# Two causal convolutions as matrix products: narrower loads for the second, split loads for the first, and kernel copies made group by group

## The chip, the cores and the metric

The kernel runs on one core of one Trainium2 chip. The metric is the device time of one execution in microseconds (us). The core has TensorE (PE: matrix products; PEld: its weight loads), VectorE (DVE), ScalarE (ACT), GpSimd (POOL) and SyncE (SP, which here issues transfers), and 16 DMA engines that move data.

## The reference, cut to what matters

```python
q, k, v = (einsum('blh,dh->bdl', u, W) + b for (W, b) in ((Wq, bq), (Wk, bk), (Wv, bv)))
k  = causal_conv(k, k_kernel)  + k_D * k          # first convolution, per channel, 512 taps
kv = k * v
y  = causal_conv(kv, ssm_kernel) + D * kv         # second convolution
x  = layernorm(u + (y * q) @ Wo.T + bo)
h  = square(relu(x @ W_fc.T)); y2 = h @ W_proj.T
x  = layernorm(x + spikes(y2) / 5)                # five threshold steps on y2
```

There are 16 sequences of 512 tokens and 256 channels; the hidden layer has 1024 units. The reference does the convolutions by FFT; only the result is wanted.

## The kernel before, in words

**Convolution as matrix product.** For each channel a causal convolution with 512 taps is a triangular Toeplitz matrix (each row is the row above, moved by one tap). It is never stored whole. A "window" tile of a channel has 128 partitions and 512 columns, and its partition p holds the taps moved right by p; TensorE uses 128 columns of it at a time as weights. Each number is kept as two float16 parts, so a channel has two windows.

**Groups, halves, steps.** The 256 channels are cut into 32 groups of 8 (`NG`, `G`), each in two halves of four channels. Step s of the first stage computes: a quarter (four of the 16 sequences) of the projection of q, k, v for the next 32 channels (line 666, 96 matmuls; not in the last four steps), the first convolution of group s (line 688, 96 matmuls) and the second convolution of group s-1 (line 688, 96 more). TensorE does them in this order.

**Where windows come from.** A prepared row of taps lies in `kpad_dram`, in 16 copies (`NCOPY`) so that 16 partitions can be read at once from different places. `spread(piece)` (line 293) makes the 16 copies from `ksplit_dram` for 32 channels (four groups) at a time: two transfers of 1024 KB, one for each convolution. `load_windows(conv, half, g)` (line 305) reads 64 partitions of one half, each partition from an address one element before its neighbour's: one transfer of 512 KB. VectorE then sets the part above the diagonal to zero (`mask`, line 975), and the other 64 partitions are a copy of the first 64, moved 64 columns to the right. For the first convolution ScalarE makes this copy (line 442; in the last four groups VectorE makes one half, line 983), for the second VectorE does (line 992).

**Buffers.** The first convolution's windows have two places (even and odd groups), the second's one place, and two in the last four groups. So a load for the second convolution waits until the same half of the group before has been used by TensorE (`c2_half`).

**What sets the order.** Each engine has one program, written out in order, and semaphores join them. SP issues all window loads and spreads on one queue. In step s it issues the load of weights and one `spread` (each fourth step, if pieces are left), then, each after its wait, the two first convolution loads of group s+2 (waiting for `c1_half` of group s) and the two second convolution loads of group s (waiting for `c2_half` of group s-1). VectorE's order in step s is: product with q of group s-2 (line 1018), both masks of the first convolution's group s+1, both masks and both copies of the second convolution's group s-1, three reads of the projection (lines 951 and 954), product with v (line 1012). At the start VectorE also splits u into two parts (line 937), between other work, and GpSimd splits two of the eight pieces (line 584).

**The second stage** (output projection, norms, the hidden layer, the spikes) comes after the last step and touches none of the changed lines.

Of the kernel before, what the change touches and what calls it, by code (L numbers as in the profile page):

```python
# [13 lines left out]
P = 128  # L14
B, L, D, F = 16, 512, 256, 1024
# [5 lines left out]
CH = 32  # L21
NC = D // CH
G = 8
GPC = CH // G
NG = D // G
HG = G // 2
HP = P // 2
ROWS = P + D * 2 * L
NCOPY = 16
SLICE = CH * 2 * L  # L30
EARLY = 4
NU = 8
UP = TOK // NU
BOTH = 4
EPS = 1e-5
X1S = 2.0 ** 10
# [35 lines left out]
def build(nc, uT, u, wcat, wk_n, wv_n, bias, bo, k1, k2, kd1, kd2, woT, wfT, wpT, out):  # L72
# [11 lines left out]
    with ExitStack() as ctx:  # L84
# [32 lines left out]
        def part(kb, dt, pattern=None, **dims):  # L117
# [83 lines left out]
            sem(n) for n in ("kpad_zero", "kpad_hi", "kpad_lo", "kpad_head", "ksplit_out", "w16_out"))  # L201
        kpad_out = [sem(f"kpad_out{n}") for n in range(NC)]

# [3 lines left out]
            sem(n) for n in ("t_zero", "c1_masked", "c2_masked", "c1_copied", "c2_copied"))  # L207
        c1_copied_dve, c1_half, c2_half = (sem(n) for n in ("c1_copied_dve", "c1_half", "c2_half"))

# [46 lines left out]
        def shifted(windows):  # L256
# [3 lines left out]
            return t[HP:P, :, HP:L], t[0:HP, :, 0:L - HP]  # L260

# [16 lines left out]
        def _(sp):  # L278
# [5 lines left out]
            for n in range(NU):  # L284
                sp.dma_start(u_st[:, :, n * UP:(n + 1) * UP],
                             uT.rearrange("(t p) n -> p t n", p=P)[:, :, n * UP:(n + 1) * UP]).then_inc(ld_u[n], 16)
            def spread(piece):

                at, n = piece * SLICE, SLICE // NCOPY
                for conv in range(2):  # L290
                    src = ksplit_dram[conv, at:at + SLICE].rearrange("(r n) -> r n", n=n)
                    dst = kpad_dram[conv, :, P + at:P + at + SLICE].rearrange("k (r n) -> r k n", n=n)
                    sp.dma_start(dst, src.unsqueeze(1).to_broadcast([NCOPY, NCOPY, n])).then_inc(kpad_out[piece], 16)

            def load_windows(conv, half, g):


                row = HG * 2 * L
                first = kpad_dram[conv, 0, P + (2 * g + half) * row:]
                if g % GPC == 0 and conv == 0 and half == 0:  # L300
                    sp.wait_ge(kpad_out[g // GPC], 32)
                second_place = conv == 1 and g >= NG - GPC and g % 2 == 0
                slot = 6 + half if second_place else 4 + half if conv else g % 2 * 2 + half
                windows = windows_of(conv, g % PAIR, half, g >= NG - PAIR)
                sp.dma_start(windows[0:HP].rearrange("p c a n -> p (c a n)"),
                             bass.AP(first.tensor, first.offset, [[ROWS - HP // NCOPY, NCOPY], [-1, HP // NCOPY], [1, row]])
                             ).then_inc(t_in[slot], 16)

# [11 lines left out]
            sp.wait_ge(ksplit_out, 32)  # L320
            spread(0)
            sp.wait_ge(kpad_head, 16)
            sp.wait_ge(kpad_out[0], 32)
            for conv, g in ((0, 0), (0, 1), (1, 0)):
                for half in range(2):
                    load_windows(conv, half, g)
            for piece in range(1, EARLY):
                spread(piece)

# [10 lines left out]
            for s in range(NG):  # L340
                chunk = s // GPC + 2
                if s % GPC == 0 and chunk < NC:
                    sp.wait_ge(proj, GPC * (chunk - 1))
                    load_w(chunk, chunk % 2)
                if s % GPC == 0 and s // GPC + EARLY < NC:
                    spread(s // GPC + EARLY)
                if s == NG - GPC:
# [509 lines left out]
        def _(dve):  # L857
# [16 lines left out]

            nc.vector.memset(T[HP:P].rearrange("p k c a n -> p (k c a) n")[:, :, 0:HP], 0.0).then_inc(t_zero, 1)
            link(nc.vector.memset(part_max[:, :], 0.0))

# [85 lines left out]
            def mask(conv, s, g, half):  # L963

                if conv == 0:
                    dve.wait_ge(t_in[s % 2 * 2 + half], 8 * (g - s % 2) + 16)
                elif isinstance(g, int) and g >= NG - GPC:

                    nth = (g - (NG - GPC)) // 2 + 1
                    dve.wait_ge(t_in[4 + half] if g % 2 else t_in[6 + half],  # L970
                                16 * (NG - GPC + nth if g % 2 else nth))
                else:
                    dve.wait_ge(t_in[4 + half], 16 * (g + 1))
                tri = windows_of(conv, s, half, final(g))[0:HP].rearrange("p c a n -> p (c a) n")[:, :, 0:HP]
                nc.vector.tensor_tensor(tri, tri, causal[0:HP, 0:HP].unsqueeze(1).to_broadcast([HP, 2 * HG, HP]),  # L975
                                        ALU.mult).then_inc((c1_masked, c2_masked)[conv], 1)
# [18 lines left out]
            dve.wait_ge(t_zero, 1)  # L995
            for quarter in range(GPC):
# [44 lines left out]
            for s in range(PAIR):  # L1041
                step(s, NG - PAIR, s < GPC, NC - 2)
                if s == GPC - 1:
                    nc.vector.memset(T2[HP:P].rearrange("p k c a n -> p (k c a) n")[:, :, 0:HP], 0.0
                                     ).then_inc(t_zero, 1)
                    dve.wait_ge(t_zero, 2)
                if s == PAIR - 2:
# [147 lines left out]
```

## Time and profile before

| | |
|---|---|
| time, median of 3 runs | 957.03 us (953.26 to 958.75) |
| the profiled execution's own time | 956.07 us |
| its span, first to last instruction | 954.3 us |
| PE / DVE / ACT / POOL busy | 80% / 73% / 54% / 42% |
| granted TensorE clock, mean | 0.926 |

The span has a first stage up to about 490 us, in which the DMA engines are busy for most of the time, and a second stage, in which they are nearly idle. Lines named in the profile, such as L688, are lines of the kernel before. `arena` is the one large tile in which windows, weights and data lie; `ps` is the matmul output memory; `qy` holds u first and then q and y. "issue" as a releaser means that an engine waited for nothing that the profile shows. Executions of this kernel differ by about half a per cent.

### The profile page before, as it was taken

Reading aid. Unit: us, or ns where it says so; the run is one execution under the profiler, and the core shown is the slowest. Engines: PE = TensorE matmul, PEld = TensorE weight load, DVE = VectorE, ACT = ScalarE, POOL = GpSimd, SP = SyncE. Lnnn points to the kernel's source line nnn. Section 1 sums busy time; section 2 is a strip of 40 time slices with the busy share of each in tenths; the row PEclk is TensorE's granted clock in tenths of the full one; section 3 lists DMA queues with packets and bytes.
Section 4 is the critical chain, followed back from the end, with each engine's and each line's share of the span. In section 5 each row is a group of like instructions: output and inputs, shape, how many; then the busy total and the mean of one; then the engine's idle time right before and its main releaser. Section 6 shows DMA issues by size and latency. Waiting matters only on the chain.

```text
span 954.3 us, 26601 instructions
## 1 busy us (share of the span) xinstructions
PE 764.2 (80%) x11392; PEld 564.0 (59%) x11392; DVE 698.8 (73%) x1087; ACT 516.9 (54%) x560; POOL 397.3 (42%) x307
## 2 busy tenths in 40 slices
PE   0086877777857878776476999999999999999993
PEld 0086877777857868776464555555555555555541
DVE  6982666556464655666575689999999999999886
ACT  2474755566563665543332565665655566665662
POOL 0361222212221222221014677666666777666642
PEclk9998898899888998988776999999999999999997
DMA  9899697979885878779931001111111101111001
GB/s 341 305 277 284 149 255 172 246 169 240 178 181 118 180 159 178 175 165 197 239 90 37 8 1 45 44 44 44 44 44 44 38 10 40 44 44 45 23 22 45
DMA packets 39294, 118.37 MB, mean 124 GB/s; under 512 B 3872, under 2 KB 23200, under 8 KB 31008
## 3 DMA queue, kind: packets, MB, share of 16 engines
q1 hardware_dynamic: 37824, 114.71, 47.1%
q10 hardware_dynamic: 1376, 2.23, 0.6%
q8 instruction: 81, 1.33, 0.6%
q14 instruction: 13, 0.11, 0.0%
HBM read 106.69 MB, written 27.01 MB: 140 GB/s over the span
## 4 chain that ended last, share of the span: by engine, by line
PE 29%; DVE 22%; DMA 20%; POOL 15%; issue 12%; ACT 2%; SPq 0%; DVEq 0%; POOLq 0%; ACTq 0%
DMA arena<-kpad_dram 17%; POOL arena L612 12%; PE ps L688 11%; DVE arena L1127 7%; PE ps L666 5%; PE ps L784 5%; PE ps L791 4%; DVE arena L992 2%; DVE arena L1084 2%; DVE arena L1124 2%; PE ps L765 2%; DVE arena L1103 2%; DVE arena L975 1%; DVE arena L1109 1%; PE ps L746 1%
## 5 line engine op out<-in xcount | busy, mean ns | idle before, releaser
L688 PE MATMUL ps<-arena 128*128 128x64 f16 (+3 forms) x6144 | 190.1, 187 | 85.2 <-DVE arena L992 42.4
L688 PEld LDWEIGHTS ps<-arena 128*128 128x128 f16 x6144 | 185.2, 101 | 88.7 <-issue 87.3
L442 ACT ACTIVATE arena<-arena 64x3584 f16<-64x3584 f16 x60 | 188.6, 3182 | 54.7 <-DVE arena L975 54.7
L666 PE MATMUL ps<-arena 128*128 128x96 f16 x3072 | 147.9, 213 | 72.5 <-DVE arena L937 51.1
L666 PEld LDWEIGHTS ps<-arena 128*128 128x128 f16 x3072 | 142.3, 102 | 75.2 <-issue 68.9
L612 POOL TENSOR_TENSOR arena<-arena 128x512 f16<-128x512 f32 x128 | 178.8, 1429 | 14.6 <-ACT arena L494 14.2
L975 DVE TENSOR_TENSOR arena<-arena 64x512 f16<-64x512 f16 x128 | 65.0, 515 | 154.6 <-DMA arena<-kpad_dram 154.4
L791 PE MATMUL ps<-arena 128*128 128x512 f16 x768 | 173.2, 379 | 2.7 <-POOL arena L612 2.7
L784 PE MATMUL ps<-arena 128*128 128x512 f16 x768 | 170.8, 379 | 0.9 <-issue 0.9
L571 POOL TENSOR_TENSOR arena<-arena 128x512 f16<-128x512 f32 x32 | 42.8, 1339 | 282.3 <-ACT arena L436 282.3
L1116 DVE TENSOR_TENSOR arena<-arena 128x512 f32<-128x512 f32 x128 | 137.6, 1128 | 10.4 <-POOL arena L612 9.0
L490 ACT ACTIVATE arena<-ps,read_factor 128x512 f32<-128x512 f32 x128 | 88.0, 687 | 79.5 <-PE ps L784 62.6
L791 PEld LDWEIGHTS ps<-arena 128*128 128x128 f16 x768 | 73.9, 98 | 90.4 <-POOL arena L612 9.5
L784 PEld LDWEIGHTS ps<-arena 128*128 128x128 f16 x768 | 74.4, 98 | 86.9 <-issue 1.4
L1127 DVE SCALAR_TENSOR_TENSOR arena<-ps,stair_at,arena 128x512 bf16<-128x512 f32 x128 | 96.1, 751 | 4.5
L494 ACT ACTIVATE arena<-arena 128x512 f16<-128x512 f32 x128 | 79.3, 623 | 29.2 <-DVE arena L1116 28.0
L478 ACT ACTIVATE arena<-arena 128x256 f32<-128x256 f32 x128 | 66.3, 589 | 35.2 <-DVE arena L1095 34.7
L616 POOL TENSOR_TENSOR arena<-arena,eps 128x4 f32<-128x4 f32 x32 | 11.7, 366 | 137.1 <-DVE arena L1089 137.1
L992 DVE COPY arena<-arena 64x3584 f16<-64x3584 f16 x64 | 67.7, 1097 | 1.0
L436 ACT ACTIVATE arena<-arena 128x512 f16<-128x512 f32 x32 | 20.1, 630 | 84.0 <-DVE arena L951 83.9
L765 PE MATMUL ps<-arena 128*128 128x256 f32 x256 | 63.0, 403 | 1.2 <-ACT arena L471 1.2
L578 POOL TENSOR_TENSOR arena<-arena 128x512 f16<-128x512 f32 x32 | 38.8, 1211 | 56.0 <-ACT arena L452 56.0
(94 smaller groups left out, 707.5 us busy)
## 6 DMA issues: line engine op xcount, KB each, us to landing
arena<-kpad_dram SPq DMA_DIRECT2D x128, 512.0 KB, 6.8
kpad_dram<-ksplit_dram SPq DMA_DIRECT2D x16, 1024.0 KB, 12.3
qy<-in_uT SPq DMA_DIRECT2D x8, 1024.0 KB, 17.3
arena<-in_u SPq DMA_DIRECT2D x16, 512.0 KB, 4.3
out<-arena SPq DMA_DIRECT2D x16, 512.0 KB, 3.0
arena<-in_k SPq DMA_DIRECT2D x2, 512.0 KB, 4.6
ksplit_dram<-arena ACTq DMA_DIRECT2D x2, 512.0 KB, 3.9
arena<-in_wfT SPq DMA_DIRECT2D x1, 1024.0 KB, 12.6
```

The lines of the kernel that those rows point to most:

```text
L442: nc.scalar.activation(*shifted(windows_of(0, s, half)), ACT.Copy).then_inc(c1_copied, 1)
L490: nc.scalar.activation(relu_h[:, f], PH[:, f % 2], ACT.Relu, scale=read_factor[:, 4:5]).then_inc(relu_ready, 1)
L494: nc.scalar.activation(h16[:, 0, f], h_square[:, f % 4], ACT.Copy).then_inc(h_hi, 1)
L612: nc.gpsimd.tensor_tensor(h16[:, 1, f], h_square[:, f % 4], h16[:, 0, f], ALU.subtract).then_inc(h_lo, 1)
L666: last = nc.tensor.matmul(o, u16[:, x, t, tok:tok + P], wcur[:, r, w, t], start=(k == 0), stop=(k == 3 * DT - 1))
L688: last = nc.tensor.matmul(out[:, ch * COL + delta * B:(ch + 1) * COL], win[:, delta * P:(delta + 1) * P], data(xp, ch)[:, 0:cols], start=( ...
L765: last = nc.tensor.matmul(PW[:, j // 2, (j % 2) * D:(j % 2 + 1) * D], yT[:, t, j * P:(j + 1) * P], wo[:, t], start=(t == 0), stop=(t == DT ...
L784: last = nc.tensor.matmul(PH[:, f % 2], wf16[:, w, t, f * P:(f + 1) * P], x16[:, r, x, t], start=(k == 0), stop=(k == 3 * DT - 1))
L791: return nc.tensor.matmul(PD[:, t], wp16[:, w, f, t * P:(t + 1) * P], h16[:, h, f], start=first, stop=last)
L992: nc.vector.tensor_copy(*shifted(windows_of(1, s, half, final(g)))).then_inc(c2_copied, 1)
L1116: nc.vector.tensor_tensor(h_square[:, f % 4], relu_h[:, f], relu_h[:, f], ALU.mult).then_inc(square_ready, 1)
L1127: ins = nc.vector.scalar_tensor_tensor(c, y, stair_at[:, n:n + 1], c, ALU.is_gt, ALU.add)
```

## The change

Three things are changed.

1. The second convolution's windows are loaded in 32 partitions (`QP`) and not 64, one transfer of 256 KB for a half. VectorE masks a smaller triangle, copies partitions 0 to 31 to 32 to 63, moved by 32 columns (the new `shifted_quarter`, counted by `c2_widened`), and then makes the copy to partitions 64 to 127 as before.
2. Each load of the first convolution's windows (still 64 partitions) is two transfers of two channels and not one of four.
3. `spread` makes the copies of one group and not four. Three groups are spread before the first window loads, five right after them, and from then on one group is spread in each of the steps 0 to 23, eight groups ahead (`AHEAD`). A run of one copy is then 1 KB long and not 4 KB.

```diff
-SLICE = CH * 2 * L
-EARLY = 4
+SLICE = G * 2 * L
+AHEAD = 8
+NKP = 2 * AHEAD
+PIECES = 2
...
+        def shifted_quarter(windows):
+            t = windows.rearrange("p c a n -> p (c a) n")
+            return t[QP:HP, :, QP:L], t[0:QP, :, 0:L - QP]
...
-            def spread(piece):
-                at, n = piece * SLICE, SLICE // NCOPY
+            def spread(g):
+                at, n = g * SLICE, SLICE // 16
...
-                if g % GPC == 0 and conv == 0 and half == 0:
-                    sp.wait_ge(kpad_out[g // GPC], 32)
+                if conv == 0 and half == 0:
+                    sp.wait_ge(kpad_out[g % NKP], 32 * (g // NKP + 1))
...
-                sp.dma_start(windows[0:HP].rearrange("p c a n -> p (c a n)"),
-                             bass.AP(first.tensor, first.offset, [[ROWS - HP // NCOPY, NCOPY], [-1, HP // NCOPY], [1, row]])
-                             ).then_inc(t_in[slot], 16)
+                parts, pieces = (QP, 1) if conv else (HP, PIECES)
+                run, c = row // pieces, HG // pieces
+                for n in range(pieces):
+                    sp.dma_start(windows[0:parts, n * c:(n + 1) * c].rearrange("p c a n -> p (c a n)"),
+                                 bass.AP(first.tensor, first.offset + n * run,
+                                         [[ROWS - parts // NCOPY, NCOPY], [-1, parts // NCOPY], [1, run]])
+                                 ).then_inc(t_in[slot], 16)
...
-            spread(0)
+            for g in range(3):
+                spread(g)
             sp.wait_ge(kpad_head, 16)
-            sp.wait_ge(kpad_out[0], 32)
             for conv, g in ((0, 0), (0, 1), (1, 0)):
                 for half in range(2):
                     load_windows(conv, half, g)
-            for piece in range(1, EARLY):
-                spread(piece)
+            for g in range(3, AHEAD):
+                spread(g)
...
-                if s % GPC == 0 and s // GPC + EARLY < NC:
-                    spread(s // GPC + EARLY)
+                if s + AHEAD < NG:
+                    spread(s + AHEAD)
...
+            nc.vector.memset(T[QP:HP, 4:6].rearrange("p k c a n -> p (k c a) n")[:, :, 0:QP], 0.0).then_inc(t_zero, 1)
...
-                tri = windows_of(conv, s, half, final(g))[0:HP].rearrange("p c a n -> p (c a) n")[:, :, 0:HP]
+                n = QP if conv else HP
+                tri = windows_of(conv, s, half, final(g))[0:n].rearrange("p c a n -> p (c a) n")[:, :, 0:n]
...
                 for half in range(2):
                     dve.wait_ge(c2_masked, 2 * g + half + 1)
+                    nc.vector.tensor_copy(*shifted_quarter(windows_of(1, s, half, final(g)))).then_inc(c2_widened, 1)
+                for half in range(2):
+                    dve.wait_ge(c2_widened, 2 * g + half + 1)
                     nc.vector.tensor_copy(*shifted(windows_of(1, s, half, final(g)))).then_inc(c2_copied, 1)
```

VectorE's order in a step, from the masks of the first convolution's windows on (a row is line, operation, output and inputs, partitions x elements, and a count where rows repeat). Before:

```order
L975 TENSOR_TENSOR arena<-arena 64x8x64 x4
L992 COPY arena<-arena 64x8x448 x2
L951 SCALAR_TENSOR_TENSOR arena<-ps,read_factor,arena 128x512
L954 TENSOR_TENSOR arena<-ps,arena 128x128x4
L954 TENSOR_TENSOR qy<-ps,arena 128x128x4
L1012 SCALAR_TENSOR_TENSOR arena<-ps,read_factor,arena 128x512
L1018 SCALAR_TENSOR_TENSOR qy<-ps,read_factor,qy 128x512
```

After:

```order
L991 TENSOR_TENSOR arena<-arena 64x8x64 x2
L991 TENSOR_TENSOR arena<-arena 32x8x32 x2
L1008 COPY arena<-arena 32x8x480 x2
L1011 COPY arena<-arena 64x8x448 x2
L966 SCALAR_TENSOR_TENSOR arena<-ps,read_factor,arena 128x512
L969 TENSOR_TENSOR arena<-ps,arena 128x128x4
L969 TENSOR_TENSOR qy<-ps,arena 128x128x4
L1031 SCALAR_TENSOR_TENSOR arena<-ps,read_factor,arena 128x512
L1037 SCALAR_TENSOR_TENSOR qy<-ps,read_factor,qy 128x512
```

Two of the four masks have become smaller, and two copies of 32 partitions stand between them and the two copies of 64; nothing else has moved.

SP's queue from the first spread on, up to the first steps (`kpad_dram` written is a spread, `arena` from `kpad_dram` a window load, from `w_dram` weights). Before:

```order
L293 DMA kpad_dram<-ksplit_dram 16x16x2048 x2
L305 DMA arena<-kpad_dram 64x1x4096 x6
L293 DMA kpad_dram<-ksplit_dram 16x16x2048 x6
L311 DMA arena<-w_dram 128x384
L293 DMA kpad_dram<-ksplit_dram 16x16x2048 x2
L305 DMA arena<-kpad_dram 64x1x4096 x14
```

After:

```order
L303 DMA kpad_dram<-ksplit_dram 16x16x512 x6
L318 DMA arena<-kpad_dram 64x1x2048 x8
L318 DMA arena<-kpad_dram 32x1x4096 x2
L303 DMA kpad_dram<-ksplit_dram 16x16x512 x10
L325 DMA arena<-w_dram 128x384
L303 DMA kpad_dram<-ksplit_dram 16x16x512 x2
L318 DMA arena<-kpad_dram 64x1x2048 x4
L303 DMA kpad_dram<-ksplit_dram 16x16x512 x2
L318 DMA arena<-kpad_dram 64x1x2048 x4
L318 DMA arena<-kpad_dram 32x1x4096 x2
L303 DMA kpad_dram<-ksplit_dram 16x16x512 x2
L318 DMA arena<-kpad_dram 64x1x2048 x4
```

Six smaller spreads and not two stand ahead of the first window loads, ten and not six behind them, and then two in each step, ahead of the loads that wait for TensorE.

## Rows read from the trace of the kernel before

**Rows 1.** The page: its head, then rows of its 40 slices (23.9 us each)

```profile
span 954.3 us, 26601 instructions
...
PE   0086877777857878776476999999999999999993
...
DVE  6982666556464655666575689999999999999886
...
DMA  9899697979885878779931001111111101111001
```

**Rows 2.** Windows: from:to, length, busy us of PE, PEld, DVE, ACT, POOL, PEclk, DMA share, GB/s

```profile
98.00:280.00 182.00, 145.43 (x4128) 142.65 (x4127) 106.46 (x159) 107.78 (x58) 35.59 (x29) 0.90 0.84 199
...
448.00:489.00 41.00, 26.37 (x768) 25.88 (x768) 26.58 (x33) 8.89 (x6) 4.77 (x4) 0.72 0.91 218
489.00:954.30 465.30, 433.45 (x2176) 239.42 (x2176) 405.16 (x676) 260.90 (x419) 295.41 (x224) 0.96 0.11 34
```

**Rows 3.** Waits, 98 to 448 us: total, times, longest

```profile
DVE arena L975 <- DMA arena<-kpad_dram: 132.0, 75, 3.6
...
PE ps L688 <- DVE arena L992: 30.5, 14, 7.2
PE ps L688 <- issue: 29.7, 15, 4.6
...
PE ps L666 <- issue: 16.6, 10, 7.4
```

**Rows 4.** The chain of work, 155 to 178 us: start, length, what

```profile
164.04 7.61 DMA arena<-kpad_dram
...
171.67 0.43 DVE arena L975
...
172.12 1.10 DVE arena L992
...
173.35 3.29 PE ps L688 x96
```

**Rows 5.** Timeline, 157 to 178 us, TensorE and the SP queue

```profile
157.26 2.65 PE L688 MATMUL ps<-arena 128*128 128x64 f16 x96
...
158.69 18.50 SPq L305 DMA_DIRECT2D arena<-kpad_dram  x8
...
161.36 2.65 PE L688 MATMUL ps<-arena 128*128 128x64 f16 x96 [1.45 <-DVE arena L992]
...
168.73 2.65 PE L688 MATMUL ps<-arena 128*128 128x64 f16 x96
```

**Rows 6.** Line 305, window loads of 98 to 448 us, issue to landing

```profile
DMA to landing us min/median/max: 4.7/6.5/15.0
```

**Rows 7.** VectorE, 51 to 98 us

```profile
93.02 0.42 DVE L975 TENSOR_TENSOR arena<-arena 64x512 f16<-64x512 f16 x1 [14.06 <-DMA arena<-kpad_dram]
95.55 1.09 DVE L975 TENSOR_TENSOR arena<-arena 64x512 f16<-64x512 f16 x3 [2.12 <-DMA arena<-kpad_dram]
```

**Rows 8.** The chain at the start, 36 to 98 us

```profile
37.27 8.52 DMA kpad_dram<-ksplit_dram
...
53.41 3.57 DVE arena L975
...
78.20 17.33 DMA arena<-kpad_dram
```

**Rows 9.** The page, DMA issues: count, KB each, median us to landing

```profile
out<-arena SPq DMA_DIRECT2D x16, 512.0 KB, 3.0
```

**Rows 10.** TensorE, 86 to 99 us

```profile
89.65 1.08 PE L688 MATMUL ps<-arena 128*128 128x64 f16 x36 [1.16 <-issue]
97.91 1.28 PE L688 MATMUL ps<-arena 128*128 128x64 f16 x29 [7.17 <-DVE arena L992]
```

**Rows 11.** TensorE, 446 to 487 us

```profile
448.16 6.83 PE L688 MATMUL ps<-arena 128*128 128x64 f16 x188 [7.01 <-DVE arena L992]
...
459.81 4.72 PE L688 MATMUL ps<-arena 128*128 128x64 f16 x123 [3.33 <-DVE arena L992]
```

More of the change, by code:

```diff
@@ L27 @@
 HP = P // 2
+QP = P // 4
 ROWS = P + D * 2 * L
 NCOPY = 16
-SLICE = CH * 2 * L
-EARLY = 4
+SLICE = G * 2 * L
+AHEAD = 8
+NKP = 2 * AHEAD
 NU = 8
@@ L201, in build @@
             sem(n) for n in ("kpad_zero", "kpad_hi", "kpad_lo", "kpad_head", "ksplit_out", "w16_out"))
-        kpad_out = [sem(f"kpad_out{n}") for n in range(NC)]
+        kpad_out = [sem(f"kpad_out{n}") for n in range(NKP)]
         t_in = [sem(f"t_in{n}") for n in range(8)]
@@ L207, in build @@
             sem(n) for n in ("t_zero", "c1_masked", "c2_masked", "c1_copied", "c2_copied"))
-        c1_copied_dve, c1_half, c2_half = (sem(n) for n in ("c1_copied_dve", "c1_half", "c2_half"))
+        c1_copied_dve, c1_half, c2_half, c2_widened = (
+            sem(n) for n in ("c1_copied_dve", "c1_half", "c2_half", "c2_widened"))
         ld_wcur = [sem(f"ld_wcur{r}") for r in range(2)]
@@ L292, in spread @@
                     dst = kpad_dram[conv, :, P + at:P + at + SLICE].rearrange("k (r n) -> r k n", n=n)
-                    sp.dma_start(dst, src.unsqueeze(1).to_broadcast([NCOPY, NCOPY, n])).then_inc(kpad_out[piece], 16)
+                    sp.dma_start(dst, src.unsqueeze(1).to_broadcast([16, NCOPY, n])).then_inc(kpad_out[g % NKP], 16)
             def load_windows(conv, half, g):
@@ L965, in mask @@
                 if conv == 0:
-                    dve.wait_ge(t_in[s % 2 * 2 + half], 8 * (g - s % 2) + 16)
+                    dve.wait_ge(t_in[s % 2 * 2 + half], 8 * PIECES * (g - s % 2) + 16 * PIECES)
                 elif isinstance(g, int) and g >= NG - GPC:
@@ L973, in mask @@
                     dve.wait_ge(t_in[4 + half], 16 * (g + 1))
-                tri = windows_of(conv, s, half, final(g))[0:HP].rearrange("p c a n -> p (c a) n")[:, :, 0:HP]
-                nc.vector.tensor_tensor(tri, tri, causal[0:HP, 0:HP].unsqueeze(1).to_broadcast([HP, 2 * HG, HP]),
+                n = QP if conv else HP
+                tri = windows_of(conv, s, half, final(g))[0:n].rearrange("p c a n -> p (c a) n")[:, :, 0:n]
+                nc.vector.tensor_tensor(tri, tri, causal[0:n, 0:n].unsqueeze(1).to_broadcast([n, 2 * HG, n]),
                                         ALU.mult).then_inc((c1_masked, c2_masked)[conv], 1)
@@ L991, in windows2 @@
                     dve.wait_ge(c2_masked, 2 * g + half + 1)
+                    nc.vector.tensor_copy(*shifted_quarter(windows_of(1, s, half, final(g)))).then_inc(c2_widened, 1)
+                for half in range(2):
+                    dve.wait_ge(c2_widened, 2 * g + half + 1)
                     nc.vector.tensor_copy(*shifted(windows_of(1, s, half, final(g)))).then_inc(c2_copied, 1)
             dve.wait_ge(id_done, 2)
-            dve.wait_ge(t_zero, 1)
+            dve.wait_ge(t_zero, 2)
             for quarter in range(GPC):
@@ L1045, in _ @@
                                      ).then_inc(t_zero, 1)
-                    dve.wait_ge(t_zero, 2)
+                    nc.vector.memset(T2[QP:HP].rearrange("p k c a n -> p (k c a) n")[:, :, 0:QP], 0.0
+                                     ).then_inc(t_zero, 1)
+                    dve.wait_ge(t_zero, 4)
                 if s == PAIR - 2:
```

## The prediction

> **What bounds the kernel now.** I read the page's slices first. In the first half of the span no engine is full: PE shows 7 and 8, DVE 5 and 6, while DMA shows 8 and 9; in the second half PE shows 9 and DMA 1 [rows 1]. The table by stage says the same in us: of the 182 us from 98 to 280 PE works 145.4, DVE 106.5 and the DMA engines 84%; from 489 to the end PE works 433 of 465 us and DMA 11% [rows 2]. All that the change touches lies before 489 us, so the last 465 us stay as they are, and the question is how soon the first stage ends.
>
> Next, who waits there. From 98 to 448 us DVE waits 132.0 us for window loads. PE waits 30.5 us for the second copy of DVE (L992), 14 times, and 46.3 us (29.7 + 16.6) for nothing that the profile shows [rows 3]. So a landing becomes a wait of PE in half the steps, and in the other half PE is held by something of its own.
>
> Then the chain, to see what a step consists of: 7.61 us from the issue of a second-convolution load to its landing, mask 0.43, first copy 1.10, then PE's 96 matmuls, 3.29 there and 2.65 in the step before, whose end lets the next load go [rows 4, 5]. That ring is 11.8 to 12.4 us. PE starts the first second-convolution block at 97.91 and the 28th at 448.16 [rows 10, 11]: 350.25 / 27 = 13.0 us a step. The ring explains most of it; PE's own 145.4 / 14 steps = 10.4 us is below it [rows 2].
>
> Why does a load take 7.6 us when the fastest of all took 4.7 [rows 6]? The queue. The first of a step's four loads leaves at 158.69 [rows 5], as the first half of the block that began at 157.26 ends; the fourth lands at 164.04 + 7.61 = 171.65 [rows 4]. Two loads that queue together land 95.55 - 93.02 = 2.53 us apart [rows 7]. So a load is 2.5 us of transfer and some 4.7 - 2.5 = 2.2 us that overlaps with the next one's, and four in a row are 4 x 2.5 + 2.2 = 12.3 (12.96 measured).
>
> **Part 1: half of the partitions for the second convolution.** What it gives: no row shows a load of 32 partitions. If its 2.53 us is pure transfer, half the bytes take 1.27, and the fourth load lands 2.5 us sooner; if it is all a cost for each transfer, nothing. I take 2.5, because the row that it is nearest to, the two landings 2.53 apart, is at a rate of 512 KB / 2.53 us = 207 GB/s, and the stage as a whole also moves 199 to 218 GB/s with 84 to 91% of the DMA time [rows 2]: the queue is busy with bytes. The Trainium skill (SBUF — State Buffer, Door 1: The DMA port swizzle) says that partitions 0 to 31 and 0 to 63 reach the same 8 ports and get the same rate, about 218 GB/s, and advises 32 over 64; by it a load of 256 KB is an estimated 1.2 us. The trace agrees on the rate of the 64 (207 GB/s); of the 32 no run here shows it.
>
> What it costs lies on the same chain, between mask and first copy: both widenings are written ahead of both copies. Two copies of 3584 elements take 2.09 us (the chain has the first at 1.10); two of 3840 elements are 2.09 x 3840 / 3584 = 2.24. The one mask on the chain has half the elements of one that takes 0.43: between 0.21 and 0.43, I take 0.28. So +2.24 - 0.15 = +2.1 us against -2.5: a step that is gated so becomes 0.4 us shorter (bounds: 2.1 longer if the load gains nothing, 0.5 shorter). Where PE is held by itself the step gains nothing. With 14 of 27 steps gated: 14 x 0.4 = **5.6 us, I take 5** (0 to 11, the last if all 27 are). DVE's own work rises from 106.5 / 14 = 7.6 to about 7.6 + 2.24 - 0.3 = 9.5 us a step, below the 13; behind the widenings stand the three reads of the projection, which free PE's next block. They come at the same distance after the second copy as now, so they move with the chain and not beyond it.
>
> **Part 2: two transfers for a load of the first convolution.** Same bytes, two more issues in each half, 0.5 us each on SP. Both go out while the first one moves (1.27 us), so I cost it at nothing. What hides it is that the loads queue; without a queue it would be the second issue, 0.5 us a half.
>
> **Part 3: spreading by group.** The bytes are the same; when they move is not. At the start: PE waits 7.17 us until 97.91 [rows 10], because a load issued at 78.20 is 17.33 us under way [rows 8], behind spreads of 1024 KB issued before it. One such pair at the start took 8.52 us to land, 6.3 without the 2.2 [rows 8], so a quarter is 1.6. After the change 12 transfers of 256 KB (10, and 2 of step 0) stand where 8 of 1024 KB did: 6 x 1.6 = 9.6 us and not 4 x 6.3 = 25. They are through before 78. The loads then land as any pair does, the second at about 84; masks, widenings and copy (0.43 + 0.56 + 2.24 + 1.10) let PE start at about 88.5. But PE is busy until 89.65 + 1.08 = 90.73 [rows 10], so the gain is 97.91 - 90.73 = **7 us** (9 if PE's unexplained stalls ahead shrink too).
>
> Before that, the first windows: now one spread pair must have landed before the loads leave, and the second mask can start only at 53.41 and then takes 3.57 us, beside GpSimd's work, where others take 0.42 [rows 7, 8]. With three groups in front (4.8 us, the fixed part hidden behind the second and third) the second load lands at about 37 + 4.8 + 5.1 + 2.2 = 49, so VectorE, free at 51.7, is done with both masks at 52.5 and not 57.0. VectorE's next split of u then meets the same GpSimd work, so of 4.4 us I take **2** (bounds 0 and 4.4).
>
> In the steps themselves a spread pair is 1.6 us in the queue in each of 24 steps, 6.3 in each of four before. It goes out right after the step's last load, when the queue runs empty; with 2 x 2.5 + 2 x 1.27 + 1.6 = 9.2 us a step the queue has room. Its runs are 1 KB, not 4. The nearest row for such runs is the output, 512 KB in runs of 1 KB, landed after 3.0 us in all [rows 9]; 1.6 us for a pair is thus not far off. I cost it at nothing (bounds: 4 us gained, since the long spreads go, 10 lost).
>
> **The last steps**, 448 to 489: no projection, so PE has 26.4 us of work in 41, and DMA is at 91% [rows 2]. Waits of 7.01 and 3.33 us end at 448.16 and 459.81 [rows 11]. Before the second, six loads queue, four of them now half as long: 5 us sooner, less 2.1 for the widening. The very last load has no queue: 1.27 gained, 2.1 paid. Sum about **2 us** gained (-1 to 5).
>
> **Sum:** 7 + 2 + 5 + 2 = 16 us. The profiled execution took 956.07, so 940; the median of the runs is 957.03, 1 above it, so 941, and I say 940.
>
> **Rivals.**
> - *PE's own stalls shrink.* 46.3 us of PE's waits have no releaser [rows 3]; they may be late instructions, which come over the same DMA engines, and these get less to do. For it: in the second stage, with DMA at 11%, PE is at 93% [rows 2]. Against: the second stage also runs far fewer instructions in a us. If a third to two thirds go, 15 to 30 us more: 910 to 925.
> - *Nothing in the steps, part of it back.* The start gains its 9 us, but each gated step loses 0.2 to 0.4 since the widening is dearer or the small spreads are in the way: 14 to 27 steps x 0.3 = 4 to 8 us back: 950 to 956.
> - *The other side: a narrow load does not land sooner by half.* If the 2.53 us has a large part that does not shrink with bytes, the pair of loads gains less than the 2.1 us that the widenings cost. At a gain of 1.0 us a step loses 1.1: 27 x 1.1 = 30 us, less 11 from start and end: 975. It decides below about 1.7 us (27 x 0.4 = 11). For it: no row of 32 partitions; against: 199 to 218 GB/s while busy. The skill's same page (The DMA setup-cost knee) states about 2 us fixed for every transfer and wants large ones; charged in the queue it would make this change slower. The trace puts that cost outside the queue: four loads took 12.96, not 4 x 4.7 = 18.8.
>
> **How the numbers follow.** Forecast 0.55 (its own range 930 to 950), stalls shrink 0.22, given back 0.12, slower load 0.11. A change below 0.5% (about 5 us) can't be told from none here. Faster than 952: forecast and stalls, and a little of the third, 0.79. Within 952 to 962: 0.10. Slower: 0.11. The range leaves out the outer half of the stalls' case and the slow one: 918 to 956.
>
> **What would show it.** After the change: the first long wait of VectorE (14.06) gone and PE's second convolution beginning near 89; the chain with a load of 5 to 5.5 us and four vector pieces behind it; a step of 12.6; landings of narrow loads 1.3 apart; minimum of a narrow load near 3.5. Wrong would be: that minimum above 4.3; a spread that lands later than 6 us in the steps and loads behind it; PE's wait for L1011 above 40 us; PE's unexplained waits far from 46.

## The result, and the profile after

The changed kernel takes 924.84 us (median of 4 runs, 921.52 to 927.61) against 956.38 before on the same chip: a ratio of 0.967 (95% interval 0.963 to 0.971). Run again later on another chip it took 924.25, ratio 0.964 (0.961 to 0.968). The forecast was 940: the direction was right, the time lies in the range of 918 to 956, but the gain is 32 us where 16 were worked out.

The page of the profiled execution; its rows answer to [rows 1], and a slice is 23.1 us now:

```profile
span 922.5 us, 26794 instructions
...
PE   0088878888867878865539999999999999999993
...
DVE  6987777777757767788955899999999999999886
...
DMA  9976777776767775678300011100111110011001
```

The first stage is over 29 us sooner (460 and not 489), a little over a slice; DVE shows 7 where it showed 5 and 6, DMA 7 where it showed 8. The stages, as in [rows 2] (from:to, length, busy us of PE, PEld, DVE, ACT, POOL, clock, DMA share, GB/s):

```profile
86.00:418.00 332.00, 267.98 (x7684) 262.90 (x7685) 251.37 (x357) 199.01 (x107) 68.00 (x54) 0.91 0.72 169
418.00:460.00 42.00, 24.72 (x768) 24.36 (x766) 37.02 (x52) 10.83 (x7) 5.70 (x5) 0.78 0.59 155
460.00:922.50 462.50, 430.08 (x2176) 237.04 (x2176) 403.80 (x664) 258.84 (x418) 294.44 (x223) 0.96 0.11 34
```

Where the time went can be read off three marks in each trace, the starts of TensorE's first, 28th and last second-convolution block:

| us | before | after | worked out |
|---|---|---|---|
| up to block 1 | 97.9 | 86.4 (-11.5) | -9 |
| 27 steps, block 1 to 28 | 350.3 (12.97 each) | 331.5 (12.28 each): -18.7 | -5 |
| block 28 to the last | 37.7 | 35.4 (-2.3) | -2 |
| from there to the end | 468.4 | 469.3 (+0.9) | 0 |

Start and end came as forecast, near enough. The steps gained almost four times as much. These marks are of one execution of each kernel; in another one of the changed kernel (`e0_changed_again`, below) the 27 steps took 333.2 us, 17.1 less than before.

The waits of these 27 steps (total, times, longest), which answer to [rows 3]:

```profile
DVE arena L991 <- DMA arena<-kpad_dram: 70.7, 63, 4.0
...
PE ps L702 <- DVE arena L1011: 43.2, 23, 7.0
...
PE ps L680 <- issue: 12.6, 6, 7.0
PE ps L702 <- issue: 7.3, 9, 1.9
```

VectorE waits 71 us for windows and not 132. TensorE waits longer for VectorE's second copy, 43.2 us and 23 times, and 19.9 us, not 46.3, for nothing that the profile shows. The chain of one step, as in [rows 4] (start, length, what):

```profile
172.83 6.10 DMA arena<-kpad_dram
...
178.96 0.29 DVE arena L991
...
179.27 2.23 DVE arena L1008 x2
...
181.52 1.10 DVE arena L1011
...
182.75 1.28 PE ps L702 x29
```

Between landing and TensorE stand four vector pieces now (mask, two widenings, copy), 0.29 + 2.23 + 1.10, 2.1 us more than before, as forecast. The widening takes 2.23 for two (2.24 worked out), the small mask 0.29 (0.28).

### The profile page after: what moved, and what is told of

Its sections match the earlier page's. It is cut to its first block, busy times and chain, and to the rows that moved or that the text cites. A ratio compares the mean times of both kernels' runs of the same rounds, so it can differ in the third digit from the quotient of the medians.

```text
span 922.5 us, 26794 instructions
## 1 busy us (share of the span) xinstructions
PE 755.7 (82%) x11392; PEld 556.8 (60%) x11392; DVE 759.0 (82%) x1153; ACT 517.5 (56%) x560; POOL 396.0 (43%) x307
## 3 DMA queue, kind: packets, MB, share of 16 engines
q10 hardware_dynamic: 1376, 2.23, 0.7%
## 4 chain that ended last, share of the span: by engine, by line
DVE 35%; PE 26%; POOL 15%; DMA 14%; issue 8%; ACT 1%; SPq 0%; DVEq 0%; POOLq 0%; ACTq 0%
POOL arena L626 13%; DMA arena<-kpad_dram 13%; PE ps L702 10%; DVE arena L1008 7%; DVE arena L1148 7%; PE ps L798 5%; PE ps L805 4%; PE ps L680 4%; DVE arena L1011 3%; DVE u_maxima L899 2%; DVE arena L1105 2%; DVE arena L1145 2%; PE ps L779 2%; DVE arena L1124 2%; DVE arena L1130 1%
## 5 line engine op out<-in xcount | busy, mean ns | idle before, releaser
L702 PE MATMUL ps<-arena 128*128 128x64 f16 (+3 forms) x6144 | 183.9, 185 | 66.9 <-DVE arena L1011 57.4
L702 PEld LDWEIGHTS ps<-arena 128*128 128x128 f16 x6144 | 179.2, 100 | 70.2 <-issue 67.8
L680 PE MATMUL ps<-arena 128*128 128x96 f16 x3072 | 148.3, 213 | 64.4 <-DVE arena L952 49.1
L680 PEld LDWEIGHTS ps<-arena 128*128 128x128 f16 x3072 | 143.2, 102 | 66.9 <-issue 61.4
L805 PEld LDWEIGHTS ps<-arena 128*128 128x128 f16 x768 | 73.9, 98 | 90.4 <-POOL arena L626 9.4
L798 PEld LDWEIGHTS ps<-arena 128*128 128x128 f16 x768 | 74.4, 98 | 86.9 <-issue 1.4
L991 DVE TENSOR_TENSOR arena<-arena 64x512 f16<-64x512 f16 (+1 forms) x128 | 52.2, 422 | 75.5 <-DMA arena<-kpad_dram 75.1
L508 ACT ACTIVATE arena<-arena 128x512 f16<-128x512 f32 x128 | 79.3, 623 | 29.2 <-DVE arena L1137 28.0
L492 ACT ACTIVATE arena<-arena 128x256 f32<-128x256 f32 x128 | 66.2, 589 | 39.9 <-DVE arena L1116 39.4
L1008 DVE COPY arena<-arena 32x3840 f16<-32x3840 f16 x64 | 71.9, 1161 | 1.0
L1011 DVE COPY arena<-arena 64x3584 f16<-64x3584 f16 x64 | 66.9, 1084 | 1.0
L779 PE MATMUL ps<-arena 128*128 128x256 f32 x256 | 60.5, 391 | 1.2 <-ACT arena L485 1.2
```

The lines of the kernel that those rows point to most:

```text
L508: nc.scalar.activation(h16[:, 0, f], h_square[:, f % 4], ACT.Copy).then_inc(h_hi, 1)
L680: last = nc.tensor.matmul(o, u16[:, x, t, tok:tok + P], wcur[:, r, w, t], start=(k == 0), stop=(k == 3 * DT - 1))
L702: last = nc.tensor.matmul(out[:, ch * COL + delta * B:(ch + 1) * COL], win[:, delta * P:(delta + 1) * P], data(xp, ch)[:, 0:cols], start=( ...
L798: last = nc.tensor.matmul(PH[:, f % 2], wf16[:, w, t, f * P:(f + 1) * P], x16[:, r, x, t], start=(k == 0), stop=(k == 3 * DT - 1))
L805: return nc.tensor.matmul(PD[:, t], wp16[:, w, f, t * P:(t + 1) * P], h16[:, h, f], start=first, stop=last)
L1008: nc.vector.tensor_copy(*shifted_quarter(windows_of(1, s, half, final(g)))).then_inc(c2_widened, 1)
```

## The experiments

**1. The three parts, one at a time, and one taken away.** The edits are the hunks of the diff above: `e1_spread_only` has the third part alone, `e2_narrow_only` the first, `e3_split_only` the second, and `e4_one_piece` is the changed kernel without the second:

```diff
-PIECES = 2
+PIECES = 1
```

At this point the theory (A) was that TensorE's unexplained waits had been late instructions, crowded out by window loads, and that fewer bytes had freed them.

> The kernel before with the third part alone: the taps are spread group by group, window loads as before. Theory A (TensorE's unexplained waits, 46.3 us between 98 and 448 us, are instructions that come late because the window loads keep the DMA engines full of bytes; the first stage gets faster as the bytes get fewer): the start gains its 9 to 11 us, the steps nothing, since the bytes in them are the same: about 946. Rival B (the small spreads themselves are what freed the steps, since no 11 us of spreading stand in the queue any more): start and some 8 us more in the steps, about 938, and unexplained waits below 35 us. Rival C (packets: the waits are due to window packets of 8 KB): as A.

> The kernel before with the first part alone: the second convolution's windows in 32 partitions, with the widening copies, spreads and first loads as before. Theory A: a quarter fewer window bytes; the unexplained waits fall from 46 to about 25 us, the steps gain 12 to 16 us and the start hardly anything: about 942. Rival B: the steps gain 5 us at most: about 950. Rival C (packet size): the packets of the narrow loads are still 8 KB, so unexplained waits stay near 40: about 950.

> The kernel before with the second part alone: each load of the first convolution in two transfers of two channels. Theory A: nothing changes, 955 to 957, unexplained waits near 46. Rival C (packet size): packets of the first convolution are 4 KB now, instructions get in between sooner, unexplained waits fall below 35 us, and the time to about 948.

> The changed kernel with the second part taken back: each load of the first convolution in one transfer of four channels. Theory A: as the changed kernel, 924 to 927 (against 957 before), unexplained waits near 20. Rival C: unexplained waits back above 30 us and 932 to 936.

| | time, us | ratio to before (95%) | TensorE's unexplained waits in 27 steps | the 27 steps |
|---|---|---|---|---|
| e1: part 3 | 941.6 | 0.983 (0.977 to 0.989) | 37.5 | 346.5 |
| e2: part 1 | 942.5 | 0.983 (0.980 to 0.987) | 32.2 | 345.4 |
| e3: part 2 | 957.8 | 1.000 (0.997 to 1.003) | 34.9 | 353.7 |
| e4: parts 1 and 3 | 930.6 | 0.972 (0.968 to 0.976) | 27.5 | 337.9 |

The last two columns are of the one profiled execution of each kernel.

Parts 1 and 3 each gain some 16 us, and their product, 0.967, is the changed kernel's ratio. Part 2 alone gains nothing. Taken away from the whole it costs 5 to 7 us between medians, but the interval of e4 begins at 0.968, where those of the changed kernel end (0.971 and 0.968); what it is worth there stays open. Part 3 works at the start. In e1 TensorE's block 1 is at 85.1 and not 97.9 (start, length, what):

```profile
85.11 3.18 PE ps L689 x96
...
88.30 6.35 DMA arena<-kpad_dram
```

12.8 us of e1's 16 are this mark. The same block of e2, with the old spreads, is still held by one load of 13.24 us:

```profile
79.17 13.24 DMA arena<-kpad_dram
...
96.77 3.68 PE ps L701 x96
```

In e2 the unexplained waits fell as theory A wanted, by a third. But in e3 they fell by 11 us and the time did not move.

The steps by themselves tell a different story from the times. Against 350.3 us before, part 1 alone took 4.9 us off the 27 steps, part 3 alone 3.8, both together 12.4, and all three 18.7 (17.1 in e0). So about half of the gain in the steps comes only with the parts together. One caution: e2's profiled execution took 947.51 us, 5 more than its median, and where these 5 lie is not known.

**2. Is it the load of the DMA engines? Is it the packets?** `e0_changed_again` is the changed kernel as it is, `e7_four_pieces` has `PIECES = 4`, and `e8_extra_8k` makes a useless copy in each step:

```diff
+                if 0 < s < NG - GPC:
+                    sp.dma_start(extra_dram[s, :, 0:4096],
+                                 ksplit_dram[s % 2, 0:262144].rearrange("(r n) -> r n", n=4096)).then_inc(extra, 16)
```

> The changed kernel again, as the base for the runs beside it. 0.967 of the kernel before (0.963 to 0.971), 922 to 928 us. If the second part (two transfers for a load of the first convolution) is really worth 5 us, it stands below the run without it (930.55, ratio 0.972).

> The changed kernel with each load of the first convolution in four transfers of one channel, packets of 2 KB and not 4. If smaller pieces as such let other packets of the queues in sooner (rival C), the gain goes on: 920 to 923, unexplained waits of TensorE below 18 us. If what counts is that loads don't get longer (theory A), 925 to 928; if the cost of each issue on SP (0.5 us, eight more in a step) is what comes next, 930 or more.

> The changed kernel with a useless copy of 512 KB from memory to memory in each of the steps 1 to 27, in 64 packets of 8 KB, issued behind the step's last window load: some 1.3 us of all 16 DMA engines in a step, so that they are as busy as before the change (about 0.81). Theory A (TensorE's unexplained waits come with the load of the DMA engines): they rise from 20 us to 30 to 45, and the time by 5 to 20 us, 930 to 945. Against it: waits stay near 20 us and the time within 3 us.

| | time, us | ratio (95%) | unexplained | waits for the second copy |
|---|---|---|---|---|
| changed, first profile | 924.84 | 0.967 (0.963 to 0.971) | 19.9 | 43.2 |
| e0: the same again | 924.25 | 0.964 (0.961 to 0.968) | 30.2 | 29.6 |
| e7: four pieces | 927.18 | 0.970 (0.965 to 0.974) | 5.2 | 59.7 |
| e8: 512 KB more a step | 930.65 | 0.972 (0.967 to 0.976) | 28.8 | 30.3 |

This table takes theory A's support away. One and the same kernel had 20 and 30 us of unexplained waits in two executions, and its time did not change; the kernel with four pieces had hardly any left (total, times, longest):

```profile
PE ps L702 <- DVE arena L1011: 59.7, 25, 4.8
...
PE ps L680 <- issue: 3.8, 1, 3.8
...
PE ps L702 <- issue: 1.4, 1, 1.4
```

and it was no faster. What TensorE does not wait in one row it waits in the other: 63, 60, 65 and 59 us in sum. So the unexplained waits seem mostly to fall into time in which the windows would not have been ready anyway. Smaller pieces bear on these waits, as rival C had it, but no gain came with it. e7 is not a clean test, though: with the additional issues on SP the fourth load leaves 1.2 us after the block that it waits for, where it leaves within 0.03 in the changed kernel, and what the missing waits may have gained can have been paid back there. The extra copy of e8 costs some 6 us (the intervals of e0 and e8 just overlap) and lifts the DMA share from 0.71 to 0.80, but the unexplained waits are not above e0's. Its time is in the range of theory A, its waits are not, and why it costs 6 us is open.

One of these waits does cost time. In every profile TensorE stands still once at the same place, ahead of the projection behind the 15th second-convolution block: 7.4 us before, 7.0 in the changed kernel, 3.8 in e4 and e7. That step takes 18.4, 18.5, 16.0 and 15.6 us, where nearly all others take 11 to 14. The change did not touch it, and no run tells what it is.

**3. What is the ring?** If TensorE's steps are set by something that is always waited for, the rows of one step tell too little. From the records of all steps I took two lengths (means over groups 2 to 26): from the end of TensorE's first half block of a group's first convolution, which lets the first of four loads go, to the landing of the fourth; and from that landing to the second convolution's block.

| us | first release to fourth landing | landing to block | two steps | rest |
|---|---|---|---|---|
| before | 13.65 | 2.33 | 25.9 | 10.0 |
| e2: part 1 alone | 11.30 | 4.36 | 25.6 | 9.9 |
| e4: parts 1 and 3 | 11.16 | 4.14 | 25.0 | 9.7 |
| changed | 10.86 | 4.03 | 24.6 | 9.7 |

The sum of the two lengths, a second-convolution block, a projection and half a first-convolution block close a ring over two steps. The rest, what is left of two steps, is TensorE's part of it, about the same in all rows; that the sum comes out is no test, since the rest is made so.

The same steps also close over one step. The fourth load leaves within 0.03 us of the end of the second-convolution block of the group before, so block, fourth load, and landing to block make a step: 3.1 + 7.5 + 2.3 us before, 3.1 + 5.1 + 4.0 in the changed kernel. Which ring holds a step is told by the fourth load. Where it stands behind the others in the queue, its landing follows from the first release (between 12.6 and 13.5 us after it in 17 of 25 groups before, whether the fourth load itself took 5.5 or 8 us), and the ring is two steps long. Where it takes little more than its least, 3.4 us, next to nothing stands ahead of it, and the ring is one step long. It took under 4.2 us in none of 25 groups before and in 9 of 25 in the changed kernel, whose steps alternate in long stretches between some 11 and some 12.5 us. `e12_widen_twice` puts a known length into both:

```diff
                 for half in range(2):
-                    dve.wait_ge(c2_widened, 2 * g + half + 1)
+                    dve.wait_ge(c2_widened, 4 * g + half + 1)
+                    nc.vector.tensor_copy(*shifted_quarter(windows_of(1, s, half, final(g)))).then_inc(c2_widened, 1)
+                for half in range(2):
+                    dve.wait_ge(c2_widened, 4 * g + 2 + half + 1)
```

> The changed kernel with each widening made twice (both, both again, then the copies): 2.24 us more between the landing and TensorE, and nothing else. Theory T (a ring over two steps: first half of the first convolution of group s, four queued loads, mask, widening, copy, second convolution of s, projection, first convolution of s+2): 1.1 us a step, 27 to 33 us, 952 to 957. Rival O (a ring over one step, as the prediction had it: second convolution, its own load, mask, widening, copy): 2.2 us a step, 50 to 60 us, 975 to 985. Rival Q (the queue's bytes bound the step and VectorE's part is hidden): under 10 us, below 934.

It took 964.65 us, ratio 1.009 (1.006 to 1.012), 40 us more than the changed kernel. Its chain at the start of the steps, and TensorE's wait for the copy in the 27 steps:

```profile
92.67 3.76 DMA arena<-kpad_dram
...
96.46 0.29 DVE arena L991
...
96.77 2.22 DVE arena L1008 x2
98.99 2.15 DVE arena L1011 x2
...
101.16 1.10 DVE arena L1014
```

```profile
PE ps L702 <- DVE arena L1014: 80.7, 26, 6.8
```

The 27 steps took 361.7 us and not 331.5 (333.2 in e0): 28.5 to 30.2 us more, 1.05 to 1.12 a step for 2.2 us on the path. That is theory T's number for the steps, and it excludes rival Q, and rival O as it was put, with a ring of one step in all steps of the changed kernel. But the trace does not show T's ring at work in e12. The fourth load takes under 4.2 us in 19 of 25 groups there (median 3.7; 3.76 in the chain above), so most steps are held by the ring of one step, 3.3 + 4.0 + 6.1 = 13.4 us. Of the 2.1 us more behind the landing 1.1 came out of the time that the fourth load had stood in the queue, and the price was uneven: the 12 shortest of 25 steps grew by 1.7 us on the mean, the 13 longest by 0.7. So half of a microsecond is the mean price of this one addition, on the way from one ring to the other. It is not shown as a rule for each step, and a further microsecond would be expected to cost more.

The time as a whole missed the expectation of 952 to 957, mostly because of the last steps, 44.1 us and not 35.4: 8.7 us for four steps, 2.2 each. There the full price is paid: VectorE is busy 39.4 of these 44.1 us, and 30.8 of 35.3 in the changed kernel, so what is added to its work has no idle time to go into.

**4. Can the ring be shortened?** `e5_half_by_half` does each half's mask, widening and copy together:

```diff
                 for half in range(2):
                     mask(1, s, g, half)
-                for half in range(2):
                     dve.wait_ge(c2_masked, 2 * g + half + 1)
                     nc.vector.tensor_copy(*shifted_quarter(windows_of(1, s, half, final(g)))).then_inc(c2_widened, 1)
-                for half in range(2):
                     dve.wait_ge(c2_widened, 2 * g + half + 1)
```

> The changed kernel with VectorE's work on the second convolution's windows written half by half: mask, widen, copy of the first half, then of the second, and not both masks, both widenings, both copies. Same instructions. Theory R (the ring: landing, mask, widening, copy, TensorE, next load; nearly each step is gated by it now): the first half is ready 2.2 to 2.4 us sooner and the second about as before, so a step gets some 0.7 to 1.3 us shorter, 27 steps 20 to 35 us, down to TensorE's own limit of 10.4 us a step and its unexplained waits: 892 to 908. Rival D (the queue's bytes bound the step, the ring only follows): no more than 5 us, 920 or above.

925.03 us, ratio 0.964 (0.960 to 0.969): nothing. That is what rival D had (the queue's bytes bound the step), but under it e12 could not have cost 40 us. The landing-to-block length fell from 4.03 to 3.22, yet a step stayed 12.28 us. The chain says what came in its place (start, length, what):

```profile
180.56 1.16 DVE arena L1007
...
181.74 1.09 DVE arena L1009
...
183.18 1.16 DVE arena L1007
...
185.48 0.75 DVE arena L966
...
186.83 0.61 DVE qy L969
...
187.48 2.58 PE ps L680 x30
```

It goes from the last widening over the copy and the reads of the projection (L966, L969) to the projection (L680) and leaves out the second convolution's block. In 16 of 25 steps the projection starts within 0.2 us of the third read's end; in the changed kernel in 12, in e0 in 13, so the difference is small. `e13_by_half_no_q` leaves the third read out of e5:

```diff
-                for s, dst in ((0, dense(ktmp[:, quarter % 2])), (1, quarter_of(vbuf[:, r], quarter)),
-                               (2, quarter_of(qy[:, bass.ds(chunk * CH * COL, CH * COL)], quarter))):
+                for s, dst in ((0, dense(ktmp[:, quarter % 2])), (1, quarter_of(vbuf[:, r], quarter)),):
```

> The half-by-half kernel (925.03) without VectorE's third read of the projection, 0.6 us a step; q is left out of the computation, so its time tells only what that read costs. Theory P, what is left of it (with the windows half by half, TensorE's next projection waits for the end of the three reads, in 16 of 25 steps to 0.2 us): the ring over two steps loses 0.6 us, so a step 0.3 and 27 steps 8 us, up to 16 if each step has the wait: 909 to 918. If the time stays within 3 us of 925, the reads are not what took the gain of the half-by-half order, and it stays open what did.

917.32 us, ratio 0.957 (0.953 to 0.961): 8 us less than e5, the 0.3 us a step that a 0.6 us read on a two-step ring gives, at the smaller end of the gain that was expected. The intervals of the two (0.960 to 0.969 for e5) just overlap, and in the profiled execution, which took longer than the median, the steps gained 4 us. So the third read took part of what the order by halves could have given; that it took all of it is not shown.

So I tried the reads ahead of the windows, alone (`e10_reads_first`) and with e5's order (`e11_reads_first_by_half`):

```diff
+                if more:
+                    if s % GPC == 0 and not (first and s == 0):
+                        dve.wait_ge(kv_lo, g)
+                    read_projection(s % GPC, (s // GPC + 1) % 2, g + GPC, chunk + s // GPC + 1)
                 if not (first and s == 0):
                     windows2((s - 1) % PAIR, g - 1)
-                if more:
-                    if s % GPC == 0 and not (first and s == 0):
-                        dve.wait_ge(kv_lo, g)
-                    read_projection(s % GPC, (s // GPC + 1) % 2, g + GPC, chunk + s // GPC + 1)
```

> The changed kernel with VectorE's three reads of the projection ahead of its work on the second convolution's windows and not behind it. Theory P (two rings tie at TensorE's next projection: its own order, which waits for the second convolution's block, and VectorE's reads, which come 2.1 us behind the copies): alone the move gains nothing, since the block is still waited for, and it puts 2 us ahead of the windows in the steps where these land early: 924 to 934. If it gains over 5 us, the reads alone bound the step.

> Both orders changed: the reads of the projection first, and the second convolution's windows half by half. Theory P: now neither ring holds the next projection back as long, a step is 0.4 to 1.0 us shorter than in the changed kernel, 27 steps 10 to 27 us: 898 to 915. If it stays at 922 or above, something else, such as the queue's bytes or the first convolution's ring over ScalarE, bounds the step, and theory P falls.

Both were plainly wrong: 1010.45 us (ratio 1.056, 1.053 to 1.059) and 1013.28 (1.059, 1.056 to 1.062), steps of 15.4 and 15.3 us. VectorE's rows of e10 (start, length; in brackets the wait before and its releaser):

```profile
172.95 0.75 DVE L966 SCALAR_TENSOR_TENSOR arena<-ps,read_factor,arena 128x512 f32<-128x512 f32 x1 [2.82 <-PE ps L680]
...
174.82 0.47 DVE L991 TENSOR_TENSOR arena<-arena 32x256 f16<-32x256 f16 x2
...
183.58 0.75 DVE L1037 SCALAR_TENSOR_TENSOR qy<-ps,read_factor,qy 128x512 f32 x1 [2.19 <-PE ps L702]
...
189.03 0.75 DVE L966 SCALAR_TENSOR_TENSOR arena<-ps,read_factor,arena 128x512 f32<-128x512 f32 x1 [4.05 <-PE ps L680]
```

The read at 189.03 waits 4.05 us for TensorE's projection, and the windows behind it in VectorE's program, which have landed, wait with it. In e11 TensorE's two waits of a step for the copies sum to 112.3 us. I had put this at 2 us in some of the steps. No version beat the changed kernel with the whole computation in it.

## Why the prediction was right, and where it was off

**The start: right, a little more than worked out** (11.5 us against 9). The 14.06 us wait of VectorE [rows 7] is 3.07 and 1.34 now, and TensorE's block 1 comes at 86.36, held by the copies and not by an old load. VectorE's and TensorE's rows:

```profile
51.47 0.74 DVE L991 TENSOR_TENSOR arena<-arena 64x512 f16<-64x512 f16 x2
...
79.46 1.23 DVE L991 TENSOR_TENSOR arena<-arena 64x512 f16<-64x512 f16 x1 [3.07 <-DMA arena<-kpad_dram]
82.03 0.82 DVE L991 TENSOR_TENSOR arena<-arena 64x512 f16<-64x512 f16 x3 [1.34 <-DMA arena<-kpad_dram]
82.88 2.22 DVE L1008 COPY arena<-arena 32x3840 f16<-32x3840 f16 x2
```

```profile
79.84 2.34 PE L702 MATMUL ps<-arena 128*128 128x64 f16 x84
86.36 3.67 PE L702 MATMUL ps<-arena 128*128 128x64 f16 x96 [4.18 <-DVE arena L1011]
```

The prediction let TensorE be busy until 90.73; it was free at 82.18, since the first projections also came sooner and its two unexplained stalls there were gone. The second mask no longer stands beside GpSimd's work: both masks take 0.74 us at 51.47, and TensorE's double block after the last split starts at 64.8 and not 67.2, so of 4.4 us some 2.5 went through (2 taken). The parts alone bear it out: block 1 moved by 12.8 us with part 3 and by 1.1 with part 1 (96.77).

**Part 1, its two sizes: right.** A narrow load takes half the transfer. In the step of the chain above VectorE's rows are

```profile
177.09 0.42 DVE L991 TENSOR_TENSOR arena<-arena 64x512 f16<-64x512 f16 x1 [2.38 <-DMA arena<-kpad_dram]
177.87 0.28 DVE L991 TENSOR_TENSOR arena<-arena 32x256 f16<-32x256 f16 x1 [0.37 <-DMA arena<-kpad_dram]
178.96 0.28 DVE L991 TENSOR_TENSOR arena<-arena 32x256 f16<-32x256 f16 x1 [0.81 <-DMA arena<-kpad_dram]
179.27 2.22 DVE L1008 COPY arena<-arena 32x3840 f16<-32x3840 f16 x2
181.52 2.09 DVE L1011 COPY arena<-arena 64x3584 f16<-64x3584 f16 x2
```

The two small masks follow landings 178.96 - 177.87 = 1.09 us apart (1.27 worked out; 2.53 for the wide ones [rows 7]). Issue to landing of all window loads of these steps, in us (min, median, max):

```profile
DMA to landing us min/median/max: 3.4/4.9/9.6
```

The least is 3.4 where it was 4.7 [rows 6]. The pair put the fourth landing 2.35 us (e2) to 2.8 us (changed) sooner, against 2.5 worked out. The Trainium skill (SBUF — State Buffer, Door 1: The DMA port swizzle) says that a transfer into 64 partitions gets the same bandwidth as one into 32; this trace, with half the bytes in about half the time, agrees.

**The steps: the term that was far too small.** The prediction wrote "a step that is gated so becomes 0.4 us shorter" and "14 x 0.4 = 5.6 us, I take 5"; "where PE is held by itself the step gains nothing". Measured: 18.7 us (17.1 in e0), 0.69 us a step over 27 steps. In the prediction's own terms:

- *The count of 14 steps.* Steps in which TensorE waits for nothing that the profile shows were counted out. But in those too the fourth load leaves at the end of the block before, and the next block stands behind its landing. Over all 25 groups the fourth load went from 7.5 to 5.1 us, 2.4 less where 2.5 were worked out.
- *The price of 2.1 us.* That is right for the chain, but the mean from landing to block rose by only 1.7 (2.33 to 4.03). Before the change TensorE was late in part of the steps (2.33 on the mean where the chain has 1.6), and it is late less often now. Why, no run isolates. 2.4 - 1.7 is the 0.7 us a step.
- *Parts 2 and 3 at nothing in the steps.* Part 1 alone took 4.9 us off the profiled steps, which is the 5 of the prediction, and part 3 alone 3.8, the gain that its bounds allowed. The other 8 to 10 us come only when the parts stand together, and the prediction has no term for that. (In e2 up to 5 us of this may be the slow execution that was profiled.) What makes them more than their sum stays open.

The ring was also taken as one step long throughout. It is that in some steps; in the others the landing follows from the first of the four loads and the ring is two steps long (experiment 3). Over two steps its two lengths went from 15.98 to 14.89 us and TensorE's part from 10.0 to 9.7: 1.1 + 0.3 over two steps is the same 0.7 a step.

**The range: right in part by luck.** The forecast's own range, 930 to 950, missed the time by 5 us. It lies within 918 to 956 because that range took in half of the stalls' case, for a mechanism that the runs do not bear out. Two signs of being wrong did come in the first profile: the wait for L1011 was 43.2 us (above 40; 29.6 in e0), and the unexplained waits were 19.9, far from 46.

**The rival of shrinking stalls: its sign and its number came, its mechanism found no support.** The unexplained waits went from 46 to 20 us, and 924.84 lies in its 910 to 925. But these waits fell by 11 us in e3, and differed by 10 between two profiles of the changed kernel, without any change of the time; more DMA work did not bring them back (e8).

**The slow rival: excluded.** It decided at a gain below 1.7 us for the pair of loads; 2.35 were measured.

**Part 2 at nothing: right alone** (e3), open in the whole (5 to 7 us between medians, intervals that touch). **Part 3 in the steps at nothing:** alone it gained 3.8 us in one execution (e1), within its bounds. A spread in the steps lands after, in us (min, median, max):

```profile
DMA to landing us min/median/max: 3.2/5.1/6.8
```

so the slowest took 6.8, a little above the 6 that was to be the alarm. No engine is seen to wait for a spread in the steps.

## What to carry to other kernels

When each step waits once for a chain through a queue and a chain of vector work, follow the ring until it closes, over as many steps as it takes, and look for a second ring beside it. Where work stands in the queue, time added behind the landing first uses up that standing time: here 2.2 us added cost 1.1 a step, and most steps then had next to no queue time left. Count the steps by the length of the load on the chain, not only by the wait of the engine at its end. Waits of an engine that end before its next gate would open are slack: don't expect them to come back as time. Measure parts together as well as alone: the steps gained 4.9 and 3.8 us by two parts alone and 12.4 by both. A copy that duplicates data inside the chip can be cheaper than loading it twice, here 1.7 to 2.1 us against 2.4, but look at what stands behind it in the same program before you reorder: moving reads of another engine's late result ahead of it cost 86 us.

## What was not expected of the hardware

TensorE's waits without a releaser varied between 3.5 (e11) and 46 us (before) among kernels, and between 20 and 30 us in two executions of the same one, without a change of the time that goes with them. And the spreads did not get cheaper in proportion: in the steps a transfer of 256 KB with runs of 1 KB landed after 5.1 us (median), one of 1024 KB with runs of 4 KB before the change after 9.3. Without the prediction's 2.2 us that overlap, an estimate, that is 2.9 for a quarter of what took 7.1. Whether the short runs or the window loads in the same queue make the difference, no run here tells.
